# Causal attention with a three-block feed on one Trainium2 core: the order of TensorE's work is planned with a charge for each change of kind, two more slots of probabilities, and the last feed in four streams

## The chip, the core and the metric

One NeuronCore of a Trainium2 chip runs the whole kernel in one launch. The metric is device time in microseconds (us), median of several runs. The core has TensorE (PE, with its weight loads as PEld), VectorE (DVE), ScalarE (ACT), GpSimd (POOL) and SyncE (SP, which here only issues transfers).

## The reference, cut to what matters

`x` is 4096 tokens by 256 channels, float32. The low-rank terms are folded into the weights.

```python
def block(x):
    a = attention(norm(x))            # 16 heads of 16 channels, causal, 4096 keys, then a projection
    x = x + norm(a)
    h = norm(x)
    for m in range(3):                # three blocks of 256x256
        y = gelu(norm(h @ W[2*m].T + b) * gamma + beta)
        h = y @ W[2*m+1].T + b + h
    return x + norm(h)
```

`norm` subtracts the mean of a row and divides by its standard deviation.

## The kernel before, in words

A first part (up to 181 us of the trace) prepares the weights, projects q, k and v, and writes q and k to memory. The change doesn't touch it. The rest is `attend_and_feed`, for which `plan` writes out an order.

**Attention.** There are 8 tiles of 512 tokens (t), each visited once for each of 4 groups of 4 heads: 32 visits. A visit goes through blocks of 128 keys, 576 blocks in all. A block has two *scores* (L904, each two matmuls side by side on 64 rows of the array, written to one of three double banks `S`), two *exps* on ACT (L872, `S` to one of 10 slots of `probs`), a mask by POOL on the diagonal (L859), and one *weigh* (L919: four heads side by side, each 32 columns of the array, summed in the bank `O`). 448 blocks are full; the 128 on the diagonal have 512, 384, 256 or 128 tokens. The trace writes a score as two records and a weigh as eight. After a visit DVE transposes and divides `O` (L1021 to L1032), and SP moves the result to `attT` (L840).

**Feed.** A tile whose four visits are done goes through eleven steps on PE: `project`, `turn_x` (transposes), and for each of three blocks `first`, `turn`, `second`. Each is done for two halves of 256 tokens, k = 0 and 1, in pieces of one matmul of 128x256 (L926, L959, L964, L968; a piece has two records in the trace) or of four transposes (L953). Every step writes the one bank `F`, and DVE must empty it (L1043, L1049, L1055) before the next step's first piece: the halves take turns. Between them DVE takes means and variances (L987, L990), an inverse root in 11 small instructions (`root`, L996 to L1006) and a scaling (L1011); ACT does the GELU on a whole tile (L879), for which it loads another table and then the one for exp again.

**The order.** `plan` is a list scheduler. It gives each item an engine, a time and what it waits for, plays the program through, and picks the ready item with the lowest rank. On PE a score has rank 0, a weigh 1, and a feed piece 0.5 once its due time (counted in scores) has come. The order so found is fixed in each engine's program. The feed of the last tile (t = 7) follows the last weigh, with nothing else beside it: this is called the tail below.

```python
        def urgent(x):
            if e == "PE" and x in due:
                return 0.5 if due[x] <= scores / 2 else 3
            return rank[x]
```

Of the kernel before, what the change touches and what calls it, by code (L numbers as in the profile page):

```python
# [23 lines left out]
P = 128  # L24
# [598 lines left out]
HB = HT // P  # L623
NS, NP = 3, 10
# [10 lines left out]
PIECES = {name: 1 if name.startswith("turn") else 4 for name in STEPS}  # L635
PIECES[STEPS[-1]] = 6
FEED_FROM, FEED_EACH = 26.0, 76.0


def feed_parts():  # L640

    parts = [("x_load", "SP", 1.0, ()), ("evac_att", "DVE", 0.8, ("project",)), ("ln_att", "DVE", 1.3, ("evac_att",)),
             ("rs_att", "DVE", 2.2, ("ln_att",)), ("add_x", "DVE", 1.5, ("rs_att", "x_load")), ("ln_x", "DVE", 1.3, ("add_x",)),
             ("rs_x", "DVE", 2.2, ("ln_x",)), ("norm_x", "DVE", 0.8, ("rs_x",)), ("copy_x", "DVE", 0.8, ("turn_x",))]
    for m in range(BLK):
        out = f"add{m}" if m < BLK - 1 else "evac_h"
        parts += [(f"evac{m}", "DVE", 0.8, (f"first{m}",)), (f"ln{m}", "DVE", 1.3, (f"evac{m}",)), (f"rs{m}", "DVE", 2.2, (f"ln{m}",)),
                  (f"norm{m}", "DVE", 0.8, (f"rs{m}",)), (f"copy{m}", "DVE", 0.8, (f"turn{m}",)), (out, "DVE", 0.9, (f"second{m}",))]  # L650
    return parts + [("ln_h", "DVE", 1.3, ("evac_h",)), ("rs_h", "DVE", 2.2, ("ln_h",)), ("result", "DVE", 1.5, ("rs_h",)), ("store", "SP", 0.5, ("result",))]
# [3 lines left out]
         **{f"turn{m}": f"norm{m}" for m in range(BLK)}, **{f"second{m}": f"gelu{m}" for m in range(BLK)}}  # L655


def plan():
# [3 lines left out]

    parts = feed_parts()
    emptied = {after[0]: name for name, _, _, after in parts if after and after[0] in STEPS}
    feed, due = [], {}
    for t in range(NT):
        mine = [(name, t, k, n) for name in STEPS for k in range(2) for n in range(PIECES[name])]
        feed += mine
        due.update({x: FEED_FROM + FEED_EACH * (t + n / len(mine)) for n, x in enumerate(mine)})
# [6 lines left out]
    for b, (v, t, c, kb, q0) in enumerate(BLOCKS):  # L676
        wide = (TT - q0) / TT
        for n in (2 * b, 2 * b + 1):
            item(("score", n), "PE", 0.02 + 0.213 * wide, [("exp", n - NS) if n >= NS else None, ("score", n - 1) if n else None,
                                                                ("k_load", c), ("q_load", v)], 0)  # L680
            item(("exp", n), "ACT", 0.165 + 0.72 * wide, [("score", n), ("exp", n - 1) if n else None,
                                                                   ("weigh", b - NP // 2) if b >= NP // 2 else None], 1)
# [3 lines left out]
        item(("weigh", b), "PE", 0.12 + 0.86 * wide, [("exp", 2 * b + 1), ("cut", 2 * b + 1) if b in DIAG else None,  # L686
                                                     ("weigh", b - 1) if b else None, ("turn_o", v - 1) if first and v else None], 1)
    for v, (t, i) in enumerate(VISITS):
        item(("turn_o", v), "DVE", 0.8, [("weigh", LAST[v])], 0)
        item(("divide", v), "DVE", 1.7, [("turn_o", v), ("moved", v - 2) if v >= 2 else None], 2)  # L690
        item(("moved", v), "SP", 1.8, [("divide", v)] + [("project", t - AS, k, 3) for k in range(2) if t >= AS], LAST[v])
# [3 lines left out]
    for m, x in enumerate(feed):  # L695
        name, t, k, n = x
        found = [feed[m - 1]] if m else []
        if n == 0:
            if m:
                found.append((emptied[feed[m - 1][0]],) + feed[m - 1][1:3])  # L700
            if name == "project":
                found += [("moved", 4 * t + i) for i in range(NG)]
            elif name.startswith("second"):
                found.append((FEEDS[name], t))
            else:
                found.append((FEEDS[name], t, k))
        item(x, "PE", 0.6 if name.startswith("turn") else 0.432, found, 2)
    for t in range(NT):
        for k in range(2):
            chain = ("result", t - 1, k) if t else None  # L710
            for name, eng, time, deps in parts:
                found = [(a, t, k, PIECES[a] - 1) if a in STEPS else (a, t, k) for a in deps]
                if name == "x_load":
                    found = [("result", t - 2, k) if t >= 2 else None]
                if eng == "DVE":
                    found.append(chain)
                    chain = (name, t, k)
                item((name, t, k), eng, time, found, FEED_FROM + FEED_EACH * t if eng == "SP" else 1 if deps[0] in STEPS else 2)
        for m in range(BLK):
            item((f"gelu{m}", t), "ACT", 4.0, [(f"copy{m}", t, k) for k in range(2)], 0)  # L720
# [12 lines left out]
    scores = 0  # L733
    while len(end) < len(after):
        now, e = min((max(free[e], min(r.values())), e) for e, r in ready.items() if r)

        def urgent(x):
            if e == "PE" and x in due:
                return 0.5 if due[x] <= scores / 2 else 3
            return rank[x]  # L740

        x = min((x for x, at in ready[e].items() if at <= now), key=lambda x: (urgent(x), ready[e][x], str(x)))
        del ready[e][x]
        scores += x[0] == "score"
        end[x] = free[e] = now + us[x]
        found[e].append(x)
        for y in users.get(x, []):
            waiting[y] -= 1
            if not waiting[y]:
                ready[engine[y]][y] = max(end[a] + (0.0 if engine[a] == engine[y] else 2.1 if engine[a] == "SP" else 0.1) for a in after[y])  # L750
# [3 lines left out]
def attend_and_feed(nc, g, d):  # L754
# [4 lines left out]
    order, _ = plan()  # L759

    done = {}
    for e in ("PE", "DVE"):
        total = [0, 0]
        for x in order[e]:
            if len(x) == 3 or len(x) == 4 and x[3] == PIECES[x[0]] - 1:
                total[x[2]] += 1
                done[x[:3]] = total[x[2]]
    place = {x[:3]: n for n, x in enumerate(x for x in order["PE"] if len(x) == 4 and x[3] == 0)}
    gelus = {x: n + 1 for n, x in enumerate(x for x in order["ACT"] if x[0] != "exp")}
    cuts = {n: m + 1 for m, n in enumerate(x[1] for x in order["POOL"])}  # L770

    with ExitStack() as ctx:
        sb = lambda n, s, t=F32: ctx.enter_context(nc.sbuf_tensor(n, s, t))
        sem = lambda n: ctx.enter_context(nc.semaphore(n))
        two = lambda n, s: [sb(f"{n}{k}", s)[(slice(None),) * len(s)] for k in range(2)]
# [10 lines left out]
        xC = sb("xC", [P, 2, 2, HB, C])  # L786
        u, y = two("uC", [P, HB, C]), two("yC", [P, HB, C])
        hT = two("hT", [P, NC, HT])
        st, mv, tmp = two("stC", [P, HB, 6]), two("mvC", [P, HB, 2]), two("tmpC", [P, 3, HB])
        rstd, nmr = two("rstdC", [P, HB]), two("nmrC", [P, HB])  # L790
# [8 lines left out]
        x_in = [[sem(f"x_in{k}{s}") for s in range(2)] for k in range(2)]  # L799
        f_ok, dve_ok, dve_chain, stored = ([sem(f"{n}{k}") for k in range(2)] for n in ("f_ok", "dve_ok", "dve_chainC", "stored"))  # L800
        LOAD = 16 * 2 * PRODUCTS
        x_halves = d["x"][0].rearrange("(t k b p) c -> t k p b c", k=2, b=HB, p=P)
        out_halves = d["out"][0].rearrange("(t k b p) c -> t k p b c", k=2, b=HB, p=P)

        def f_rows():
            return F[:, :].rearrange("p (b c) -> p b c", b=HB)

        def repeated(row):
            return row.unsqueeze(1).to_broadcast([P, HB, C])

        with nc.Block() as block:

            @block.sync
            def _(sp):
                need = sp.value_load(g["need_max"][0:1, 0:1], min_val=0, max_val=1)
                for x in order["SP"]:
# [25 lines left out]
                    elif x[0] == "x_load":  # L842
                        _, t, k = x
                        if t >= 2:
                            sp.wait_ge(dve_ok[k], done["result", t - 2, k])
                        sp.dma_start(xC[:, k, t % 2, :, :], x_halves[t, k]).then_inc(x_in[k][t % 2], 16)
                    else:
                        _, t, k = x
                        sp.wait_ge(dve_ok[k], done["result", t, k])
                        sp.dma_start(out_halves[t, k], y[k]).then_inc(stored[k], 16)  # L850
                for k in range(2):
                    sp.wait_ge(stored[k], 16 * NT)

            @block.gpsimd
            def _(pool):
                for _, n in order["POOL"]:
                    pool.wait_ge(exp_ok, n + 1)
                    tri = probs[:, n % NP, :, 0:P]
                    nc.gpsimd.affine_select(out=tri, in_=tri, compare_op=ALU.is_ge, fill=0.0, base=0,  # L859
                                            pattern=[[0, 2], [1, P]], channel_multiplier=-1).then_inc(cut_ok, 1)  # L860

            @block.scalar
            def _(act):
                for x in order["ACT"]:
# [8 lines left out]
                    else:  # L873
                        m, t = int(x[0][-1]), x[1]
                        for k in range(2):
                            act.wait_ge(dve_ok[k], done[f"copy{m}", t, k])
                        for c in range(NC):
                            col = m * NC + c
                            last = nc.scalar.activation(zT[:, c, :], zT[:, c, :], ACT.Gelu, bias=g["beta"][:, col:col + 1],  # L879
                                                        scale=g["gamma"][:, col:col + 1])  # L880
                        last.then_inc(gelu_ok, 1)

            @block.tensor
            def _(pe):
# [235 lines left out]
```

## Time and profile before

| | |
|---|---|
| median of 3 runs | 1584.68 us (1582.41 to 1588.07) |
| the profiled execution | 1590.69 us, of which its span is 1588.9 us |
| busy in the span | PE 90%, PEld 36%, DVE 40%, ACT 75%, POOL 8% |
| mean granted TensorE clock | 0.939 |
| first score, last weigh, end | 181.4, 1463.6, 1588.9 us |

In rows, a line such as L904 is a line of the kernel before, and "x8" counts records. A time in brackets is idle time of the engine just before the row, with what ended it. PEclk is the granted clock as a share of 2.4 GHz, so 0.5 is 1.2 GHz.

### The profile page before, as it was taken

How to read it: one execution, taken by the hardware profiler on the slowest of the kernel's cores; microseconds unless marked ns; L12 is line 12 of the kernel's file. 1: busy time of each engine (PE TensorE's matmuls, PEld its weight loads, DVE VectorE, ACT ScalarE, POOL GpSimd, SP SyncE). 2: the span in 40 equal slices, each digit the busy share in tenths (PEclk: the TensorE clock that was granted, in tenths of full speed). 3: DMA queues.
4: the chain of work that ended last, by engine and by line, in shares of the span. 5: the costliest groups of instructions: out<-in, count | busy, mean ns of one | idle time of the engine just before them, and what ended most of it. 6: DMA issues, size and time to landing. Idle time of an engine off the chain costs nothing.

```text
span 1588.9 us, 26355 instructions
## 1 busy us (share of the span) xinstructions
PE 1436.3 (90%) x8646; PEld 567.1 (36%) x8646; DVE 638.8 (40%) x2232; ACT 1183.8 (75%) x1370; POOL 131.6 (8%) x355
## 2 busy tenths in 40 slices
PE   6899379999999999999999999999999999998354
PEld 3455123433333333333333333333333333332233
DVE  3376025434633355324531453245332453131635
ACT  1365257888888888888889988888888888888010
POOL 0121122101100000000000000000000000000000
PEclk7699579999999999999999999999999999999666
DMA  5265344445432243223322332223322322210000
GB/s 136 80 211 212 98 103 125 114 113 131 119 79 77 72 101 85 67 69 94 84 71 58 92 97 57 68 77 87 78 71 60 103 61 63 54 32 11 1 0 14
DMA packets 104120, 131.99 MB, mean 83 GB/s; under 512 B 33200, under 2 KB 48560, under 8 KB 103984
## 3 DMA queue, kind: packets, MB, share of 16 engines
q1 hardware_dynamic: 97280, 124.44, 29.3%
q10 hardware_dynamic: 6704, 5.87, 1.3%
q8 instruction: 70, 1.15, 0.3%
q14 instruction: 66, 0.54, 0.1%
HBM read 105.03 MB, written 20.97 MB: 79 GB/s over the span
## 4 chain that ended last, share of the span: by engine, by line
PE 72%; ACT 6%; DVE 5%; SPq 4%; issue 3%; DMA 0%; DVEq 0%; ACTq 0%
PE O L919 29%; PE S L904 23%; PE F L926 10%; PE F L959 4%; SPq L489 3%; ACT probs L872 3%; PE F L953 2%; PE F L964 2%; ACT L872 1%; PE F L968 1%; ACT zT L879 1%; DVE zT L1049 1%; ACT L879 1%; DVE yC L1011 1%; SPq L840 1%
## 5 line engine op out<-in xcount | busy, mean ns | idle before, releaser
L872 ACT ACTIVATE probs<-S 128x1024 f32<-128x1024 f32 (+3 forms) x1152 | 1018.7, 966 | 197.1 <-PE S L904 172.9
L919 PE MATMUL O<-probs,vg 128*32 128x512 f32 (+3 forms) x4608 | 573.5, 576 | 7.2 <-DVE o_turned L1021 4.5
L904 PE MATMUL S<-q_op,k_op 64*128 64x512 f32 (+3 forms) x2304 | 476.9, 455 | 47.5 <-DMA q_op<-qk_rows 27.8
L904 PEld LDWEIGHTS S<-q_op,k_op 64*128 64x128 f32 x2304 | 198.4, 187 | 549.7 <-ACT probs L872 357.3
L859 POOL TENSOR_SCALAR_AFFINE_SELECT probs<-probs 128x256 f32<-128x256 f32 x256 | 103.5, 412 | 1167.9 <-ACT probs L872 1165.5
L1043 DVE TENSOR_TENSOR uC<-F,bffn 128x512 f32<-128x512 f32 x64 | 44.3, 692 | 339.1 <-PE F L926 210.1
L919 PEld LDWEIGHTS O<-probs,vg 128*32 128x32 f32 x4608 | 95.5, 109 | 168.4 <-issue 143.3
L926 PE MATMUL F<-wfT,hT 128*128 128x256 f32 x384 | 129.5, 436 | 6.2 <-DVEq L1044 3.1
L1055 DVE SCALAR_TENSOR_TENSOR hT<-F,b2T,hT 128x256 f32<-128x256 f32 x64 | 28.0, 480 | 184.9 <-PE F L959 184.9
L959 PE MATMUL F<-zT,wfT 128*128 128x256 f32 x256 | 84.6, 445 | 9.2 <-ACT zT L879 6.7
L926 PEld LDWEIGHTS F<-wfT,hT 128*128 128x128 f32 x384 | 63.3, 197 | 53.9 <-issue 39.7
L953 PE MATMUL F<-ident,yC 128*128 128x128 f32 x256 | 44.1, 298 | 36.4 <-DVE yC L1011 36.4
L879 ACT ACTIVATE zT<-zT,beta,gamma 128x512 f32<-128x512 f32 x48 | 36.4, 805 | 51.3 <-DVEq L1051 51.1
L1021 DVE STREAM_TRANSPOSE o_turned<-O 128x512 f32<-128x512 f32 x32 | 22.8, 713 | 118.7 <-PE O L919 118.7
L879 ACT ACT_TABLE_LOAD x22 | 28.2, 1283 | 55.6 <-DVEq L1051 55.4
L987 DVE BATCH_NORM_STATS2 stC<-uC 128x6 f32<-128x256 f32 x160 | 60.1, 418 | 14.4 <-DVEq L1045 13.9
L1011 DVE TENSOR_SCALAR yC<-uC,rstdC,nmrC 128x256 f32<-128x256 f32 x160 | 59.3, 414 | 7.0 <-DVE uC L1043 3.8
L959 PEld LDWEIGHTS F<-zT,wfT 128*128 128x128 f32 x256 | 46.0, 206 | 43.0 <-issue 35.0
L457 PE MATMUL psQ<-xnT,wqkvT 128*128 128x512 f32 x128 | 59.7, 622 | 1.2 <-ACT xnT L341 1.2
L1049 DVE COPY zT<-F 128x512 f32<-128x512 f32 x48 | 33.0, 688 | 65.4 <-PE F L953 65.4
L926 PE MATMUL F<-wpT,attT 128*128 128x256 f32 x128 | 45.5, 448 | 7.2 <-DMA attT<-o_div 6.3
L964 PE MATMUL F<-wfT,zT 128*128 128x256 f32 x128 | 42.3, 432 | 7.6 <-ACT zT L879 6.6
(95 smaller groups left out, 807.0 us busy)
## 6 DMA issues: line engine op xcount, KB each, us to landing
k_op<-qk_rows SPq DMA_DIRECT2D x1152, 64.0 KB, 2.3
qk_rows<-parts SPq DMA_DIRECT2D x32, 512.0 KB, 3.1
q_op<-qk_rows SPq DMA_DIRECT2D x256, 64.0 KB, 2.3
attT<-o_div SPq DMA_DIRECT2D x128, 32.0 KB, 2.0
xC<-in_L_attn_x SPq DMA_DIRECT2D x16, 256.0 KB, 3.1
out<-yC SPq DMA_DIRECT2D x16, 256.0 KB, 2.4
x_in<-in_L_attn_x ACTq DMA_DIRECT2D x6, 512.0 KB, 4.8
q_int<-in_L_ffn_qweights ACTq DMA_DIRECT2D x1, 1536.0 KB, 8.8
```

The lines of the kernel that those rows point to most:

```text
L457: last_mm = nc.tensor.matmul(psQ[:, m, :], g["wqkvT"][:, c, m * P:(m + 1) * P], xnT[:, u, c, :], start=(c == 0), stop=(c == NC - 1))
L859: nc.gpsimd.affine_select(out=tri, in_=tri, compare_op=ALU.is_ge, fill=0.0, base=0, pattern=[[0, 2], [1, P]], channel_multiplier=-1).then_ ...
L872: nc.scalar.activation(probs[:, n % NP, :, 0:TT - q0], S[:, n % NS, :, 0:TT - q0], ACT.Exp, scale=SCALE).then_inc(exp_ok, 1)
L879: last = nc.scalar.activation(zT[:, c, :], zT[:, c, :], ACT.Gelu, bias=g["beta"][:, col:col + 1], scale=g["gamma"][:, col:col + 1])
L904: last = nc.tensor.matmul(S[:, n % NS, a, 0:TT - q0], k_op[mine, c % RING, n % 2, kb % NB * P:(kb % NB + 1) * P], q_op[mine, v % QS, n % 2 ...
L919: last = nc.tensor.matmul(O[h * STRIP:(h + 1) * STRIP, q0:TT], vg[:, kb, col:col + STRIP], probs[:, (2 * b + h // 2) % NP, h % 2, 0:TT - q ...
L926: return nc.tensor.matmul(F[:, b * C:(b + 1) * C], src(c, b), w[:, c, :], start=(c == 0), stop=(c == NC - 1))
L953: last = nc.tensor.transpose(F[:, c * HT + b * P:c * HT + (b + 1) * P], y[k][:, b, c * P:(c + 1) * P], g["ident"][:, :])
L959: last = nc.tensor.matmul(F[:, o * HT:(o + 1) * HT], g["wfT"][:, 2 * m + 1, c, o * P:(o + 1) * P], zT[:, c, k * HT:(k + 1) * HT], start=(c ...
L964: nc.tensor.matmul(F[:, b * C:(b + 1) * C], zT[:, c, tok(b)], g["wfT"][:, 2 * m + 1, c, :], start=(c == 0), stop=False, skip_group_check=True)
L987: last = nc.vector.bn_stats(st[k][:, b, :], src[:, b, :])
L1011: last = nc.vector.tensor_scalar(y[k][:, b, :], src[:, b, :], rstd[k][:, b:b + 1], nmr[k][:, b:b + 1], ALU.mult, ALU.add)
```

## The change

It has three parts.

1. **The planner's rules for PE.** `SWITCH` charges 0.21, 0.13 or 0.2 us when PE's next item is a score, a weigh or a feed piece and the one before it was of another kind; the times of single items lose a part that stood for this. The ranks are replaced: scores are taken when at most `LOW_WATER` = 1 score is ahead of ACT or while a run of scores lasts, a weigh or a feed step that has begun goes on, and a due feed piece waits until two scores are ahead.
2. **Twelve slots of `probs`** for ten, so that exps may be six blocks ahead of the weighs.
3. **The last tile's feed in four streams** of 128 tokens. Stream 0 writes `F`, streams 1 to 3 write one bank each of `S`, which is free by then. A step no longer waits for the bank of another stream. ACT takes over the scaling before a transpose (`norm`) and the copy after it (`copy`); POOL takes over `root` in streams 1 and 3, in 12 instructions; the GELU and the store are done for each stream. The tiles before keep their two halves.

```diff
-NS, NP = 3, 10
+NS, NP = 3, 12
+LOW_WATER, FEED_WATER = 1, 2
+HOP = 0.15
+SWITCH = {"score": 0.21, "weigh": 0.13, "feed": 0.2}
+def parted(t):
+    return 4 if t == NT - 1 else 2
+def runs_on(name, t, k):
+    if name == "store":
+        return "SP"
+    if t == NT - 1 and name.startswith(("norm", "copy")):
+        return "ACT"
+    if t == NT - 1 and name.startswith("rs") and k % 2:
+        return "POOL"
+    return "DVE"
...
-        def urgent(x):
-            if e == "PE" and x in due:
-                return 0.5 if due[x] <= scores / 2 else 3
-            return rank[x]
+        def wish(x):
+            if e != "PE":
+                return rank[x]
+            ahead = scores - sum(1 for z in exp_ends[-8:] if z <= now) - max(0, len(exp_ends) - 8)
+            if x[0] == "score":
+                return 0 if kind == "score" or ahead <= LOW_WATER else 3
+            if x[0] == "weigh":
+                return 1.5 if kind == "weigh" else 2
+            if x[3] and kind == "feed":
+                return 1
+            return 1.8 if due[x] <= scores / 2 and ahead >= FEED_WATER else 4
...
-        end[x] = free[e] = now + us[x]
+        start = now
+        if e == "PE":
+            scores += x[0] == "score"
+            now_kind = x[0] if x[0] in SWITCH else "feed"
+            start += 0.0 if now_kind == kind else SWITCH[now_kind]
+            kind = now_kind
+        end[x] = free[e] = start + us[x]
...
+        def bank(t, k):
+            return F if t < NT - 1 or k == 0 else S[:, k - 1, 0, :]
...
+                    elif name.startswith("norm"):
+                        inputs_done(act, name, t, k)
+                        src = xC[:, t % 2] if name == "norm_x" else u
+                        for b in range(NB)[rows(t, k)]:
+                            last = nc.scalar.activation(y[:, b, :], src[:, b, :], ACT.Identity, bias=nmr[:, b:b + 1], scale=rstd[:, b:b + 1])
+                        last.then_inc(act_ok[k], 1)
+                    else:
+                        inputs_done(act, name, t, k)
+                        dst = hT if name == "copy_x" else zT
+                        nc.scalar.copy(dst[:, :, toks(t, k)], in_channels(t, k)).then_inc(act_ok[k], 1)
```

On PE, where tile 5's first feed block begins amid scores (`S`) and weighs (`O`), the order before goes on, behind the 843rd score:

```order
L919 MATMUL O<-probs,vg 32x512 x4
L904 MATMUL S<-q_op,k_op 128x384 x2
L953 MATMUL F<-ident,yC 128x128 x4
L904 MATMUL S<-q_op,k_op 128x256 x2
L919 MATMUL O<-probs,vg 32x512 x4
L904 MATMUL S<-q_op,k_op 128x256 x2
L904 MATMUL S<-q_op,k_op 128x128 x2
L926 MATMUL F<-wfT,hT 128x256
L904 MATMUL S<-q_op,k_op 128x128 x2
L926 MATMUL F<-wfT,hT 128x256
L904 MATMUL S<-q_op,k_op 128x512 x4
L926 MATMUL F<-wfT,hT 128x256
```

The same place of the order after the change (its lines are L1035 for scores, L1050 for weighs, L1084 and L1098 for the feed):

```order
L1035 MATMUL S<-q_op,k_op 128x512 x6
L1084 MATMUL F<-ident,yC 128x128 x4
L1050 MATMUL O<-probs,vg 32x512 x4
L1035 MATMUL S<-q_op,k_op 128x512 x2
L1035 MATMUL S<-q_op,k_op 128x384 x2
L1098 MATMUL F<-wfT,hT 128x256 x2
L1035 MATMUL S<-q_op,k_op 128x384 x2
L1035 MATMUL S<-q_op,k_op 128x256 x2
L1098 MATMUL F<-wfT,hT 128x256 x2
L1035 MATMUL S<-q_op,k_op 128x256 x2
L1035 MATMUL S<-q_op,k_op 128x128 x4
```

Scores come in twos and threes and feed pieces in twos, where they came one at a time. Over the whole order up to the last weigh, PE begins 802 runs of scores, 530 of weighs and 409 of feed pieces before, and 492, 372 and 230 after the change.

On PE at the end, behind the last weigh, before:

```order
L919 MATMUL O<-probs,vg 32x512 x8
L926 MATMUL F<-wpT,attT 128x256 x8
L953 MATMUL F<-ident,yC 128x128 x8
L926 MATMUL F<-wfT,hT 128x256 x8
L953 MATMUL F<-ident,yC 128x128 x8
L959 MATMUL F<-zT,wfT 128x256 x8
L926 MATMUL F<-wfT,hT 128x256 x8
```

And after the change:

```order
L1050 MATMUL O<-probs,vg 32x512 x8
L1098 MATMUL F<-wpT,attT 128x256 x2
L1098 MATMUL S<-wpT,attT 128x256 x6
L1084 MATMUL F<-ident,yC 128x128 x2
L1098 MATMUL F<-wfT,hT 128x256 x2
L1084 MATMUL S<-ident,yC 128x128 x2
L1098 MATMUL S<-wfT,hT 128x256 x2
L1084 MATMUL S<-ident,yC 128x128 x4
L1098 MATMUL S<-wfT,hT 128x256 x4
```

The streams write different banks, so that one stream's products stand between another's transposes.

## Rows read from the trace of the kernel before

**Rows 1.** The page's chain that ended last, shares of the span by line
```profile
PE O L919 29%; PE S L904 23%; PE F L926 10%; PE F L959 4%; SPq L489 3%; ACT probs L872 3%; PE F L953 2%; PE F L964 2%; ACT L872 1%; PE F L968 1%; ACT zT L879 1%; DVE zT L1049 1%; ACT L879 1%; DVE yC L1011 1%; SPq L840 1%
```
**Rows 2.** Stretches: attention, tail; busy us (records), PEclk, DMA share, GB/s
```profile
core 0: us, PE busy (x) PEld busy (x) DVE busy (x) ACT busy (x) POOL busy (x), PEclk, DMA share, GB/s
181.00:1464.00 1283.00, 1244.98 (x8032) 454.33 (x8032) 493.01 (x1763) 1104.41 (x1236) 103.55 (x256) 0.98 0.32 81
1464.00:1589.00 125.00, 52.94 (x160) 37.60 (x160) 61.46 (x238) 5.83 (x7) 0.00 (x0) 0.64 0.02 6
```
**Rows 3.** Timeline of PE amid attention: start us, us, what
```profile
1299.08 1.13 PE L926 MATMUL F<-wfT,hT 128*128 128x256 f32 x4
1300.14 0.49 PE L904 MATMUL S<-q_op,k_op 64*128 64x512 f32 x2
1300.56 0.70 PE L926 MATMUL F<-wfT,hT 128*128 128x256 f32 x2
1301.19 0.49 PE L904 MATMUL S<-q_op,k_op 64*128 64x512 f32 x2
1301.62 1.07 PE L919 MATMUL O<-probs,vg 128*32 128x512 f32 x8
1302.61 0.49 PE L904 MATMUL S<-q_op,k_op 64*128 64x512 f32 x2
1303.04 1.07 PE L919 MATMUL O<-probs,vg 128*32 128x512 f32 x8
1304.03 0.73 PE L904 MATMUL S<-q_op,k_op 64*128 64x512 f32 x4
...
1352.23 1.92 PE L919 MATMUL O<-probs,vg 128*32 128x512 f32 x16
```
**Rows 4.** Timeline of ACT in the same place
```profile
1304.57 3.77 ACT L872 ACTIVATE probs<-S 128x1024 f32<-128x1024 f32 x4 [0.40 <-PE S L904]
1308.67 2.85 ACT L872 ACTIVATE probs<-S 128x1024 f32<-128x1024 f32 x3 [0.33 <-PE S L904]
```
**Rows 5.** The page's group of exps, and waits: total us, times, longest
```profile
L872 ACT ACTIVATE probs<-S 128x1024 f32<-128x1024 f32 (+3 forms) x1152 | 1018.7, 966 | 197.1 <-PE S L904 172.9
...
ACT probs L872 <- PE S L904: 172.9, 280, 27.4
ACT probs L872 <- PE O L919: 19.8, 19, 2.7
```
**Rows 6.** Timeline of the tail
```profile
1462.52 1.06 PE L919 MATMUL O<-probs,vg 128*32 128x512 f32 x8 [0.75 <-ACT probs L872]
1469.84 3.37 PE L926 MATMUL F<-wpT,attT 128*128 128x256 f32 x8 [6.25 <-DMA attT<-o_div]
1499.41 0.69 DVE L1043 TENSOR_TENSOR uC<-F,bffn 128x512 f32<-128x512 f32 x1 [4.36 <-PE F L926]
1500.34 0.75 DVE L987 BATCH_NORM_STATS2 stC<-uC 128x6 f32<-128x256 f32 x2 [0.24 <-DVEq L1045]
1501.13 0.25 DVE L990 BATCH_NORM_AGGREGATE mvC<-stC 128x2 f32<-128x6 f32 x2
1501.41 0.17 DVE L996 TENSOR_SCALAR tmpC<-mvC 128x2 f32<-128x2 f32 x1
1503.39 0.16 DVE L1006 SCALAR_TENSOR_TENSOR nmrC<-mvC,rstdC 128x2 f32<-128x2 f32 x1
1519.39 0.88 DVE L1055 SCALAR_TENSOR_TENSOR hT<-F,b2T,hT 128x256 f32<-128x256 f32 x2 [7.06 <-PE F L959]
1585.57 0.69 DVE L1074 TENSOR_TENSOR yC<-yC,xC 128x512 f32<-128x512 f32 x1
```
**Rows 7.** Timeline of POOL before attention: first and last of 11 instructions, twice
```profile
32.46 0.20 POOL L82 TENSOR_TENSOR tmpA<-rstdA 128x4 f32<-128x4 f32 x1 [30.93 <-DVE rstdA L112]
35.28 0.20 POOL L95 TENSOR_TENSOR nmrA<-tmpA,rstdA 128x4 f32<-128x4 f32 x1
106.20 0.30 POOL L82 TENSOR_TENSOR tmpA<-rstdA 128x4 f32<-128x4 f32 x1 [6.55 <-DVE rstdA L112]
111.52 0.20 POOL L95 TENSOR_TENSOR nmrA<-tmpA,rstdA 128x4 f32<-128x4 f32 x1 [0.18 <-POOL rstdA L92]
```

More of the change, by code:

```diff
@@ L658, in plan, with gelu_of @@
+def gelu_of(name, t, k):
+    return (f"gelu{name[-1]}", t, k if t == NT - 1 else 0)
 def plan():
     parts = feed_parts()
[L664 removed]
+    emptied = {after[0]: name for name, _, _, after in parts if after[0] in STEPS}
     feed, due = [], {}
     for t in range(NT):
[L667 removed]
+        mine = [(name, t, k, n) for name in STEPS for k in range(parted(t)) for n in range(pieces(name, t))]
@@ L749, in plan @@
             if not waiting[y]:
-                ready[engine[y]][y] = max(end[a] + (0.0 if engine[a] == engine[y] else 2.1 if engine[a] == "SP" else 0.1) for a in after[y])
+                ready[engine[y]][y] = max(end[a] + (0.0 if engine[a] == engine[y] else 2.1 if engine[a] == "SP" else HOP) for a in after[y])
     return found, end
@@ L759, in attend_and_feed @@
     order, _ = plan()
+    parts_after = {name: after for name, _, _, after in feed_parts()}
     done = {}
-    for e in ("PE", "DVE"):
-        total = [0, 0]
+    for e in ("PE", "DVE", "ACT", "POOL"):
+        total = [0] * 4
         for x in order[e]:
-            if len(x) == 3 or len(x) == 4 and x[3] == PIECES[x[0]] - 1:
+            if len(x) == 3 and not x[0].startswith("gelu") or len(x) == 4 and x[3] == pieces(x[0], x[1]) - 1:
                 total[x[2]] += 1
                 done[x[:3]] = total[x[2]]
-    place = {x[:3]: n for n, x in enumerate(x for x in order["PE"] if len(x) == 4 and x[3] == 0)}
-    gelus = {x: n + 1 for n, x in enumerate(x for x in order["ACT"] if x[0] != "exp")}
-    cuts = {n: m + 1 for m, n in enumerate(x[1] for x in order["POOL"])}
+    place = {x[:3]: n for n, x in enumerate(x for x in order["PE"] if len(x) == 4 and x[3] == 0 and x[1] < NT - 1)}
+    gelus = {x: n + 1 for n, x in enumerate(x for x in order["ACT"] if x[0].startswith("gelu"))}
+    cuts = {n: m + 1 for m, n in enumerate(x[1] for x in order["POOL"] if x[0] == "cut")}
     with ExitStack() as ctx:
@@ L854, in _, with link @@
             @block.gpsimd
             def _(pool):
[L856 to L860, printed above, removed]
+                links = [0] * 4
+                def link(k, ins):
+                    links[k] += 1
+                    ins.then_inc(pool_chain[k], 1)
+                    pool.wait_ge(pool_chain[k], links[k])
@@ new lines, in _ @@
+                for x in order["POOL"]:
+                    if x[0] == "cut":
+                        n = x[1]
+                        pool.wait_ge(exp_ok, n + 1)
+                        tri = probs[:, n % NP, :, 0:P]
+                        nc.gpsimd.affine_select(out=tri, in_=tri, compare_op=ALU.is_ge, fill=0.0, base=0,
+                                                pattern=[[0, 2], [1, P]], channel_multiplier=-1).then_inc(cut_ok, 1)
+                    else:
+                        name, t, k = x
+                        inputs_done(pool, name, t, k)
+                        root(t, k).then_inc(pool_ok[k], 1)
@@ L1014, in _, with scaled, emptied @@
+                def scaled(t, k, src):
+                    for b in range(NB)[rows(t, k)]:
+                        last = nc.vector.tensor_scalar(y[:, b, :], src[:, b, :], rstd[:, b:b + 1], nmr[:, b:b + 1], ALU.mult, ALU.add)
+                    return last
+                def emptied(t, k, ins):
+                    link(k, ins)
+                    if t < NT - 1:
+                        dve.sem_inc(f_out, 1)
+                    dve.sem_inc(dve_ok[k], 1)
                 link(0, nc.vector.memset(o_turned[:, :, :], 0.0))
```

312 lines of the change are left out of this document (178 added, 134 removed).

## The prediction, made before the changed kernel had run

> **What bounds the kernel now.** I read the chain that ended last first. Scores and weighs, the work of attention on PE, hold 52% of it and ACT some 4% [rows 1]. The table by stretch then cuts the span in two. In attention, 1283 us long, PE is busy 1245 us, ACT 1104, and the granted clock is 0.98, so PE runs almost always at 2.4 GHz: PE is the bound, with ACT not far behind. In the tail, 125 us, nobody is busy for long: DVE 61 us, PE 53, at a mean clock of 0.64, between 1.2 and 2.4 GHz [rows 2]. There a chain of steps that take turns on one bank is the bound.
>
> What fills PE's 1245 us? The timeline gives it [rows 3]. Four records of scores last 0.73 us and two last 0.49, so a further score costs 0.24 us. Sixteen records of weighs last 1.92 and eight 1.07: 0.85 for a further weigh. Four records of a feed product last 1.13 and two 0.70: 0.43 for a further piece. But the starts lie further apart than that. A score alone is followed 0.43 us after its start (1301.19 to 1301.62), a weigh after 0.99 (1301.62 to 1302.61), a feed piece after 0.63 (1300.56 to 1301.19). So each run, whatever comes next, pays once: 0.19 us for scores, 0.14 for weighs, 0.20 for feed. At these prices the runs of the order before cost 802 x 0.19 + 530 x 0.14 + 409 x 0.20 = 308 us, a quarter of attention.
>
> **Part 1, the planner's rules.** The order loses 310 runs of scores, 158 of weighs and 179 of feed: 58.9 + 22.1 + 35.8 = 117 us. No matmul is added or removed in attention. It lies on the path, since PE is the bound. Two bounds around it: PE is idle or between rows for 38 us of the stretch [rows 2], and if all of that were waits that grow back where a change used to fill them, 79 us would be left. On the upper side the new order may also take some of these waits away, as it holds scores further ahead of need; I allow 10 us and get 127. I take 117, the value of the rows themselves.
>
> Can ACT follow? Its rows cover 1104 us [rows 2]. Exps in a row begin 0.92 us apart (3.77 less 2.85 [rows 4]) though their mean is 0.966 [rows 5], so up to 1152 x 0.046 = 53 us less is needed: 1051 to 1104. The new stretch is 1282 - 117 = 1165 us, so ACT may wait 61 to 114 us in all and hides. It waited 173 us for scores before, in 280 waits [rows 5]. The cover is thin: what is late next, once PE is this fast, is the score for ACT. Behind an ACT wait stand only further exps, and PE's next weigh wants those, so a wait there comes back on PE only when the slots ahead are used up.
>
> The trace and the Trainium skill differ on what a run pays. In the rows the second score, weigh or product of a run pays nothing but its own columns [rows 3]. The page TensorE: Matmul & The Clock Gate, section Part 3: Packing small matmuls, says that a weight load overlaps with matmuls in flight only when its row group differs; every 128-row feed piece and every weigh would then pay for its load, inside a run too, and the second score of a run as well. By the page longer runs would save nothing; by the rows they save all but the first. The sum goes by the rows.
>
> **Part 2, twelve slots.** ACT waited for a weigh to free a slot 19 times, 19.8 us in all [rows 5]. ACT isn't the bound, so I cost this at nothing; its bounds are 0 and a gain of 20 us if ACT should have become the bound. Its work is hidden by PE's 1165 us.
>
> **Part 3, four streams in the tail.** From the end of the last weigh (1462.52 + 1.06 = 1463.6) to the end are 125.3 us. The first 6.3 us, until the first product, stay: DVE divides, SP moves [rows 6]. Now each stream has its own bank, so the wait of one for another's emptying goes, and DVE becomes the engine that all share. Its work, by rows of the tail [rows 6]: an emptying of 512 elements takes 0.69 us and 0.24 until the next instruction; for 256 elements I take 0.45 + 0.24 (a DVE row of 256 from `F` takes 0.88 / 2 = 0.44), 20 of them, 13.8 us. Statistics for one block: half of 0.75, rounded up to 0.42 for the single row, 0.2 for the aggregate and two small instructions at 0.2, with gaps 1.1 us, 24 times: 26.4. A `root` has 11 instructions from 1501.41 to 1503.55, 0.195 apiece; nine remain in it, 1.76 us, 12 times on DVE: 21.1. Two additions of 128 and their wait 0.8 us, 8 times: 6.4. Scaling and adding x, 0.85 us, 8 times: 6.8. Together 74.5 us, more than the 61 of before, for the small instructions cost the same for one block as for two. With 8.4 us before its first emptying (6.3 and two pieces at the low clock, 3.37 / 4 each with a further 0.4) and 2.7 us behind its last (1585.57 + 0.69 to 1588.9), the tail can't be shorter than 86 us.
>
> It will be longer, since POOL's `root` is slow. The nearest rows are the same arithmetic ahead of attention: 11 instructions took 3.0 us with POOL alone (32.46 to 35.48) and 5.5 us beside a busy DVE (106.20 to 111.72) [rows 7]. Twelve instructions are thus 3.3 to 6.0 us against 1.76 on DVE. DVE is the busy engine of the tail, so I take 5.0, nearer to the busy rows. A stream's six roots follow one another: 6 x (5.0 - 1.8) = 19 us on the streams 1 and 3, of which the last ends the kernel. 86 + 19 = 105 us. The bounds are 86 and 125 (no gain). The gain is 20 us, 0 to 39. ACT's added work, 16 scalings, 16 copies and 12 pairs of GELUs, is far below the 80 us in which it had nothing to do; if it were late, DVE's emptyings would wait.
>
> The Trainium skill has a rule against this part. SBUF — State Buffer, section SBUF: two separate sides, says that VectorE and GpSimd share a port pair under an exclusive lock, and the loser waits for the whole instruction. By it DVE's many two-input instructions and POOL's would hold each other up; at its worst the tail would gain nothing. The two timings of rows 7, 3.0 and 5.5 us, agree with such a rule, and the sum already carries a price between them.
>
> **The sum.** 1590.7 (the profiled execution's own time) - 117 - 20 - 0 = 1453.7 us. The median of the runs shown lies 6.0 us lower, so **1447.7 us** against 1584.7, a factor of 0.914.
>
> **The rivals.**
> *A, ACT becomes the bound.* Every one of the 492 runs of scores comes so late that ACT waits 0.33 us, the shorter wait of rows 4. Then attention takes 1104 + 162 = 1266 us, a gain of 16 only, and the kernel 1549 us. For it: scores are now asked for only when at most one is ahead. Against: two or three scores come at a time, and only 280 waits belonged to 802 runs before. Chance 0.08.
>
> *B, slower.* The same place, a larger price: at each run ACT waits 172.9 / 280 = 0.62 us, as in its average wait before [rows 5], because PE is in a weigh (0.99 us) or in four feed pieces (1.9 us) when the last score is being used. Then 1104 + 305 = 1409 us, 127 more than before, less 20 in the tail: 1692 us. It decides from (1282 + 20 - 1104) / 492 = 0.40 us a run. Against: the order puts a score run ahead of other work while ACT still has one in hand, which lasts 0.92 us. Chance 0.03.
>
> *C, a run pays for each of its members.* The price would belong to each weight load and the rows 3 would be a chance pattern; attention stays, the tail gains: 1584.7 - 20 = 1565 us. This is what the rule of TensorE's page comes to. Against: three pairs of rows speak for the first alone. Chance 0.04.
>
> That the change doesn't shorten the runs is excluded by the order itself.
>
> **How the numbers follow.** The forecast has 0.83, A 0.08, C 0.04, B 0.03, and 0.02 are left for what I don't see. Within the forecast, gains of 79 to 127 us and 0 to 39 in the tail reach from 1419 to 1506; both ends at once are unlikely, and the range is 1425 to 1490. A measurement of this kernel can tell about 0.3% (5 us) from no change. All cases but B are faster by more, so faster 0.95, same 0.02, slower 0.03.
>
> **What the profile should show.** Attention from 1282 to about 1165 us at a clock near 1; PE's busy time there down by some 100 us with the same records; the starts behind a run of two scores 0.67 us apart and of three 0.91; ACT over 90% busy with its waits for scores below 114 us. In the tail DVE busy over 70 us of about 105, POOL rows of 0.2 to 0.55 us, and no PE row that waits for another stream's emptying. The forecast is wrong if the runs are longer in the trace and PE's stretch isn't shorter (C), or if ACT's idle time behind scores grows (A, B), or if the tail ends with POOL's instructions on the chain for more than 19 us.

## The result, and the profile after

The changed kernel takes 1453.77 us (median of 4 runs, 1452.23 to 1458.97) against 1586.38 us before: a ratio of 0.917, 95% interval 0.9136 to 0.9204. Forecast were 1447.7 us, or 0.914, in a range of 1425 to 1490. The profiled execution took 1458.97 us with a span of 1457.2, so against the profiled one before (1590.69) it is 131.7 us shorter. 137 had been forecast.

The page's chain that ended last, after the change, answers to [rows 1]. PE's share of weighs and scores went from 52 to 48%, that of ACT's exps (L990) from 3 to 6%.

```profile
PE O L1050 28%; PE S L1035 20%; PE F L1098 9%; ACT probs L990 6%; SPq L489 4%; PE F L1088 2%; PE F L1084 2%; ACT L1000 2%; ACT L990 1%; ACT zT L1000 1%; PE S L1098 1%; PE F L1102 1%; SPq L926 1%; DVE stC L1120 0%; DVE uC L1187 0%
```

The two stretches of the changed kernel, attention and tail, with the columns of [rows 2]:

```profile
181.00:1367.00 1186.00, 1142.98 (x8032) 473.72 (x8032) 494.22 (x1763) 1084.96 (x1236) 103.51 (x256) 0.98 0.35 88
1367.00:1457.00 90.00, 43.82 (x192) 34.59 (x192) 58.79 (x260) 26.04 (x57) 28.09 (x144) 0.75 0.03 8
```

From here on, attention is the time from the first score's start to the start of DVE's last transpose of `O`, and the tail what follows. Attention went from 1282.2 us (181.41 to 1463.66) to 1185.2 (181.66 to 1366.82), 97 less; the tail from 125.2 to 90.4, 35 less. So both parts gained, but not in the shares of the forecast, 117 and 20. In attention PE has the same 8032 records in 102 us less; ACT is busy for 91% of it instead of 86%.

The timeline of PE amid attention after the change, as [rows 3]:

```profile
645.64 0.73 PE L1035 MATMUL S<-q_op,k_op 64*128 64x512 f32 x4
646.31 1.28 PE L1050 MATMUL O<-probs,vg 128*32 128x128 f32 x16
647.52 0.73 PE L1035 MATMUL S<-q_op,k_op 64*128 64x512 f32 x4
648.18 1.13 PE L1098 MATMUL F<-wfT,hT 128*128 128x256 f32 x4
649.25 0.73 PE L1035 MATMUL S<-q_op,k_op 64*128 64x512 f32 x4
649.91 1.92 PE L1050 MATMUL O<-probs,vg 128*32 128x512 f32 x16
651.76 0.96 PE L1035 MATMUL S<-q_op,k_op 64*128 64x512 f32 x6
652.66 1.13 PE L1098 MATMUL F<-wfT,hT 128*128 128x256 f32 x4
653.72 1.06 PE L1050 MATMUL O<-probs,vg 128*32 128x512 f32 x8
654.71 0.99 PE L1035 MATMUL S<-q_op,k_op 64*128 64x512 f32 x6
655.64 1.92 PE L1050 MATMUL O<-probs,vg 128*32 128x512 f32 x16
```

A run of two scores is followed 0.66 us after its start, one of three after 0.90 (651.76 to 652.66), two weighs after 1.85, two feed pieces after 1.06: the prices of [rows 3] again, in the longer runs. One row differs. The three scores at 654.71 last 0.99 and are followed after 0.93: the third had to wait for ACT to leave its bank.

The waits of ACT after the change (total us, times, longest), as the last lines of [rows 5]:

```profile
ACT probs L990 <- PE S L1035: 101.3, 121, 27.4
ACT probs L990 <- PE O L1050: 18.4, 16, 2.7
```

In both kernels the longest of the waits for scores, 27.4 us, lies ahead of the first exp and so outside attention. Inside it ACT waited 145.5 us in 279 waits before, and 73.9 us in 120 waits after.

### The profile page after: what moved, and what is told of

It is laid out like the page before. It is cut to its first block, busy times and chain, and to the rows that moved or that the text cites. A ratio compares the mean times of both kernels' runs of the same rounds, so it can differ in the third digit from the quotient of the medians.

```text
span 1457.2 us, 26427 instructions
## 1 busy us (share of the span) xinstructions
PE 1325.1 (91%) x8678; PEld 583.4 (40%) x8678; DVE 637.3 (44%) x2254; ACT 1184.6 (81%) x1420; POOL 159.6 (11%) x499
## 4 chain that ended last, share of the span: by engine, by line
PE 63%; ACT 10%; issue 5%; SPq 5%; DVE 3%; POOL 1%; DMA 1%; DVEq 0%; ACTq 0%; POOLq 0%
PE O L1050 28%; PE S L1035 20%; PE F L1098 9%; ACT probs L990 6%; SPq L489 4%; PE F L1088 2%; PE F L1084 2%; ACT L1000 2%; ACT L990 1%; ACT zT L1000 1%; PE S L1098 1%; PE F L1102 1%; SPq L926 1%; DVE stC L1120 0%; DVE uC L1187 0%
## 5 line engine op out<-in xcount | busy, mean ns | idle before, releaser
L990 ACT ACTIVATE probs<-S 128x1024 f32<-128x1024 f32 (+3 forms) x1152 | 999.2, 968 | 124.6 <-PE S L1035 101.3
L1050 PE MATMUL O<-probs,vg 128*32 128x512 f32 (+3 forms) x4608 | 539.9, 572 | 5.1 <-DVE o_turned L1163 2.4
L1035 PE MATMUL S<-q_op,k_op 64*128 64x512 f32 (+3 forms) x2304 | 409.8, 435 | 52.0 <-DMA q_op<-qk_rows 30.7
L1035 PEld LDWEIGHTS S<-q_op,k_op 64*128 64x128 f32 x2304 | 188.5, 188 | 426.9 <-ACT probs L990 310.2
L1050 PEld LDWEIGHTS O<-probs,vg 128*32 128x32 f32 x4608 | 111.1, 109 | 211.7 <-issue 187.4
L1187 DVE TENSOR_TENSOR uC<-F,bffn 128x512 f32<-128x512 f32 (+1 forms) x60 | 40.4, 673 | 253.1 <-PE F L1098 143.9
L1098 PE MATMUL F<-wfT,hT 128*128 128x256 f32 x348 | 95.5, 404 | 0.5 <-ACT hT L1012 0.5
L1193 DVE SCALAR_TENSOR_TENSOR hT<-F,b2T,hT 128x256 f32<-128x256 f32 (+1 forms) x60 | 25.7, 470 | 148.5 <-PE F L1088 148.4
L1098 PEld LDWEIGHTS F<-wfT,hT 128*128 128x128 f32 x348 | 60.6, 191 | 29.2 <-issue 21.9
L1088 PE MATMUL F<-zT,wfT 128*128 128x256 f32 (+1 forms) x240 | 63.0, 396 | 6.0 <-ACT zT L1000 5.7
L357 ACT ACTIVATE qf<-psQ,bqk 128x512 f32<-128x512 f32 x32 | 21.9, 684 | 34.4 <-PE psQ L457 33.9
L1084 PE MATMUL F<-ident,yC 128*128 128x128 f32 x232 | 38.6, 288 | 10.2 <-ACT yC L1007 9.9
L1000 ACT ACTIVATE zT<-zT,beta,gamma 128x512 f32<-128x512 f32 (+1 forms) x66 | 42.4, 690 | 0.6
L1098 PE MATMUL F<-wpT,attT 128*128 128x256 f32 x116 | 33.4, 413 | 6.4 <-DMA attT<-o_div 6.3
L1098 PE MATMUL F<-wfT,zT 128*128 128x256 f32 x116 | 35.1, 412 | 3.0 <-ACT zT L1000 2.6
```

Source lines behind the costliest of these rows:

```text
L990: nc.scalar.activation(probs[:, n % NP, :, 0:TT - q0], S[:, n % NS, :, 0:TT - q0], ACT.Exp, scale=SCALE).then_inc(exp_ok, 1)
L1000: last = nc.scalar.activation(zT[:, c, at], zT[:, c, at], ACT.Gelu, bias=g["beta"][:, col:col + 1], scale=g["gamma"][:, col:col + 1])
L1035: last = nc.tensor.matmul(S[:, n % NS, a, 0:TT - q0], k_op[mine, c % RING, n % 2, kb % NB * P:(kb % NB + 1) * P], q_op[mine, v % QS, n % 2 ...
L1050: last = nc.tensor.matmul(O[h * STRIP:(h + 1) * STRIP, q0:TT], vg[:, kb, col:col + STRIP], probs[:, (2 * b + h // 2) % NP, h % 2, 0:TT - q ...
L1084: last = nc.tensor.transpose(into[:, o0:o0 + P], y[:, b, c * P:(c + 1) * P], g["ident"][:, :])
L1088: last = nc.tensor.matmul(into[:, o * wide:(o + 1) * wide], g["wfT"][:, 2 * m + 1, c, o * P:(o + 1) * P], zT[:, c, at], start=(c == 0), st ...
```

## The experiments

The stretches are those of one profiled execution of each kernel, measured as above. Three kernels have the same order of attention and the same exps (changed, root_dve, tail_dve); they lie within 3.0 us of each other there, which tells how exact a stretch is. Each ratio is to executions of the kernel before that go with that kernel (their medians are 1584.5 to 1587.0 us), with its 95% interval.

| kernel | time, us | ratio to before | attention | tail |
|---|---|---|---|---|
| before | 1586.4 | 1 | 1282.2 | 125.2 |
| changed | 1453.8 | 0.917 (0.914 to 0.920) | 1185.2 | 90.4 |
| rules_alone | 1495.7 | 0.943 (0.940 to 0.946) | 1189.6 | 125.4 |
| tail_alone | 1563.2 | 0.985 (0.982 to 0.988) | 1287.9 | 92.5 |
| ten_slots | 1465.8 | 0.924 (0.921 to 0.927) | 1194.5 | 90.5 |
| no_charge | 1508.0 | 0.951 (0.948 to 0.954) | 1234.4 | 89.8 |
| half_exp_before | 1574.2 | 0.992 (0.989 to 0.995) | 1268.5 | 125.5 |
| half_exp_after | 1421.6 | 0.896 (0.893 to 0.899) | 1150.8 | 90.2 |
| root_dve | 1465.5 | 0.924 (0.921 to 0.926) | 1182.7 | 100.8 |
| tail_dve | 1479.7 | 0.932 (0.930 to 0.934) | 1185.7 | 114.0 |
| no_tables | 1426.1 | 0.899 (0.896 to 0.902) | 1154.5 | 89.3 |
| tuned | 1434.1 | 0.904 (0.902 to 0.906) | 1165.0 | 85.9 |

**One part alone: rules_alone.** The kernel before with the charges and the ranks of the change, some other item times of the planner with them.

```diff
-            return rank[x]          # a score 0, a weigh 1, a due feed piece 0.5
+            ...                     # wish(x) and SWITCH of the change
```

> The kernel before with the planner's charges and ranks alone (ten slots, last feed in two halves). PE begins 495 runs of scores, 378 of weighs and 234 of feed before the last weigh, 307, 152 and 175 fewer than before. Price-per-run theory: attention shorter by the 97 us that the change showed, give or take 8, tail as before at 125; about 0.938 of before. Rival (the slots carry part of the gain, ACT waits for slots again): attention gains only 60 to 80, ratio 0.95 or more.

The two stretches of this run:

```profile
180.00:1370.00 1190.00, 1141.72 (x8032) 471.83 (x8032) 492.31 (x1763) 1086.05 (x1236) 103.71 (x256) 0.99 0.34 88
1370.00:1495.00 125.00, 53.14 (x160) 37.72 (x160) 61.24 (x238) 5.83 (x7) 0.00 (x0) 0.64 0.02 6
```

Attention gained 92.6 us, within the 89 to 105 that I had expected, and the tail stayed; the ratio, 0.943, is a little above my 0.938. The rules make nearly all of attention's gain. The range that I gave was the 97 us already measured, give or take 8, and not the price: by the price, 307, 152 and 175 runs fewer are worth 58.3 + 21.3 + 35.0 = 115 us. So this kernel too lacks some 22 us of it, as the changed one lacks 20.

**One part alone: tail_alone.** The changed kernel with the old ranks and item times and ten slots.

```diff
-NS, NP = 3, 12
+NS, NP = 3, 10
...
-        x = min(..., key=lambda x: (wish(x), ready[e][x], str(x)))
+        x = min(..., key=lambda x: (urgent(x), ready[e][x], str(x)))
```

> The changed kernel with the old charges, ranks and ten slots, so only the four streams in the tail are new. Attention as before at 1282 us (within 8), tail 90 us as in the changed kernel; ratio 0.978. Rival (the tail gained because the clock was carried over from a denser attention, not by its streams): tail above 105, ratio above 0.987.

The tail alone:

```profile
1468.00:1560.00 92.00, 46.45 (x192) 33.42 (x192) 59.06 (x260) 26.12 (x57) 28.91 (x144) 0.78 0.03 8
```

It takes 92.5 us behind a slow attention too, so its gain is its own and not that of a denser attention ahead of it. Attention was 5.7 us longer than before, within the 8 us that I had allowed: the old rules wrote a slightly other order here (12 more runs, 1.9 us by their price). The ratio is 0.985 where I had expected 0.978.

**The slots: ten_slots.**

```diff
-NS, NP = 3, 12
+NS, NP = 3, 10
```

> The changed kernel with ten slots of probabilities; the planner writes an order for ten, with 487, 380 and 228 runs. If the slots were worth nothing as forecast: within 0.3% of the changed kernel. If ACT is close to being the bound: 5 to 20 us slower, with more waits of ACT for a weigh than 18 us.

12 us slower than the changed kernel by the medians (8 between the two profiled executions), with intervals that lie apart. Attention is 9.3 us longer. ACT's waits for a weigh grew:

```profile
ACT probs L990 <- PE O L1050: 29.3, 32, 2.5
```

So the slots are worth something, where I had forecast nothing. The number of runs is the same (1095 for 1094): what they buy is room for ACT. How much is less sure. rules_alone has ten slots as well, and its attention is only 4.4 us longer than that of the changed kernel, 2.2 of which its 13 further runs explain. The two pairs put the slots' worth in attention at 2 to 9 us.

**The charge: no_charge.**

```diff
-SWITCH = {"score": 0.21, "weigh": 0.13, "feed": 0.2}
+SWITCH = {"score": 0.0, "weigh": 0.0, "feed": 0.0}
```

> The changed kernel with the three charges at zero, the new ranks kept: 549, 459 and 235 runs, 57, 87 and 5 more than the changed kernel. By the price of a run that is 57 x 0.19 + 87 x 0.14 + 5 x 0.20 = 24 us more. If the order must also know when PE is late, ACT waits more than 101 us for scores, and it is 24 to 80 us slower. Rival (the ranks do it all, the charge is only bookkeeping): within 5 us of the changed kernel.

Attention is 49 us longer. The 149 further runs account for 24 of it, and ACT's waits for scores are longer by 60:

```profile
ACT probs L990 <- PE S L1035: 161.7, 251, 27.3
```

The ranks by themselves give half of attention's gain (48 of 97 us); the other half needs a planner that knows when PE will really be free. One place of the trace shows how the order fails without it. Behind one of ACT's GELUs, PE waits for ACT ahead of two single scores. In the plan's own reckoning the exps that these scores wait for had ended before PE came free:

```profile
801.24 0.38 PE L1035 MATMUL S<-q_op,k_op 64*128 64x256 f32 x2 [0.50 <-ACT probs L990]
801.94 0.33 PE L1035 MATMUL S<-q_op,k_op 64*128 64x128 f32 x2 [0.32 <-ACT probs L990]
```

**Where the missing 20 us are: half_exp_before and half_exp_after.** In both kernels an exp works on half of its columns, and what it leaves out keeps what the slot held (1.0 at the start). PE's instructions and their order stay as they are.

```diff
-nc.scalar.activation(probs[:, n % NP, :, 0:TT - q0], S[:, n % NS, :, 0:TT - q0], ACT.Exp, scale=SCALE)
+nc.scalar.activation(probs[:, n % NP, :, 0:(TT - q0) // 2], S[:, n % NS, :, 0:(TT - q0) // 2], ACT.Exp, scale=SCALE)
...
+nc.vector.memset(probs[:, :, :, :], 1.0)     # once, ahead of attention
```

> The kernel before, each exp over half of its columns only (the other half of the probabilities is a constant), so ACT cannot be late. TensorE's instructions and their order are those of before. If PE's list is the bound of attention: attention loses little, from 1282 to 1255 to 1275 us. Rival (ACT's waits and PE's are one loop and the exps were the bound in places): below 1240.

> The changed kernel with the same half exps. If the price of a run (0.19, 0.14, 0.20 us) is right, the difference between this and half_exp_before in attention is 117 us, 20 more than with whole exps, since the 20 missing are waits for ACT: attention near 1145 to 1155 us. Rival (the missing 20 lie in PE's own list or in the transfers at the start): the difference stays near 97.

Attention of the kernel before, then of the changed one, each with half exps:

```profile
180.00:1449.00 1269.00, 1238.73 (x8032) 451.65 (x8032) 491.25 (x1763) 689.96 (x1236) 102.76 (x256) 0.99 0.33 82
```

```profile
182.00:1333.00 1151.00, 1121.15 (x8032) 466.58 (x8032) 494.29 (x1763) 661.47 (x1236) 101.63 (x256) 0.98 0.37 90
```

ACT is busy for some 670 us instead of 1100. Attention falls to 1268.5 and to 1150.8 us, both within what I had expected. Their difference is 117.7 us, and the price of the runs had given 117. PE's records alone show it as well: 1238.73 less 1121.15 is 117.6. So close a match is in part luck: the prices are rounded to 0.01 us, which for 647 runs leaves 3 us either way. With whole exps 97 are left, since ACT costs the order before 14 us and the new one 34.

**What of ACT it is: no_tables.** The identity stands where the GELU stood, which needs no other table.

```diff
-last = nc.scalar.activation(zT[:, c, at], zT[:, c, at], ACT.Gelu, ...)
+last = nc.scalar.activation(zT[:, c, at], zT[:, c, at], ACT.Identity, ...)
```

> The changed kernel with the identity in place of the GELU (the GELU itself is left out), so ACT loads no table for it: 42 loads of 1.28 us, 54 us, go from ACT's 1085 in attention, at the same order of PE. If ACT is the bound in places: attention falls by a part of the 34 us that half exps gave, 10 to 30 us. Rival (a table load is hidden in the slots ahead): less than 5 us.

Attention is 30.7 us shorter, just above the 10 to 30 that I had expected and nearly the 34 that half exps gave. The group in question, from the timeline of ACT in the changed kernel:

```profile
631.58 1.28 ACT L1000 ACT_TABLE_LOAD   x1
632.88 1.52 ACT L1000 ACTIVATE zT<-zT,beta,gamma 128x512 f32<-128x512 f32 x2
634.41 1.28 ACT L990 ACT_TABLE_LOAD   x1
635.71 16.31 ACT L990 ACTIVATE probs<-S 128x1024 f32<-128x1024 f32 x20
652.30 11.34 ACT L990 ACTIVATE probs<-S 128x1024 f32<-128x1024 f32 x12 [0.29 <-PE S L1035]
```

21 times ACT leaves the exps for 4.13 us (631.58 to 635.71), 2.56 of it loads. After this pause it works through 20 exps with no wait: it is behind, and PE's order is then held to ACT's pace. Behind the 21 pauses there are 6 to 23 such exps, 12 in the median; in the kernel before, whose pauses are as long, 3 to 10, 8 in the median.

Whether the loss arises there can be read off row by row, since the changed kernel, half_exp_after and no_tables have the same 8032 records of PE in the same order. Take the 21 stretches from the beginning of a pause to the end of its exps without a wait, 313 us of attention in all. In them the changed kernel falls behind no_tables by 31.3 us, and in all the rest by nothing (it regains 0.6). Behind half_exp_after it falls by 29.5 of the 34.4 us in them. So nearly the whole loss arises behind the pauses.

**The tail, engine by engine: root_dve and tail_dve.** In root_dve the roots of streams 1 and 3 are on DVE; in tail_dve the scalings and copies as well.

```diff
-    if t == NT - 1 and name.startswith(("norm", "copy")):     # left out in tail_dve only
-        return "ACT"
-    if t == NT - 1 and name.startswith("rs") and k % 2:       # left out in both
-        return "POOL"
```

> The changed kernel with the roots of streams 1 and 3 in the tail on DVE too, none on POOL. Attention has the same order. If DVE is what the streams share, its 12 further roots of 1.76 us (21 us) lengthen the tail from 90 to 100 to 111 us. Rival (the chain of a stream bounds, and POOL's 3.3 us for a root only delay it): tail 80 to 90.

> The changed kernel with roots, scalings and copies of the tail all on DVE: only four streams with banks of their own are left of its third part. DVE then has 21 us of roots, 16 scalings of 0.45 and 16 copies of 0.65 us more, 39 us in all. If DVE is the shared bound: tail 120 to 130 us, as long as before, and the streams by themselves are worth nothing. Rival (the banks are the gain): tail 90 to 105.

The tail of root_dve, then of tail_dve:

```profile
1364.00:1464.50 100.50, 46.60 (x192) 35.42 (x192) 74.10 (x368) 26.59 (x57) 0.00 (x0) 0.73 0.02 7
```

```profile
1366.00:1479.00 113.00, 54.09 (x192) 41.61 (x192) 85.92 (x400) 10.31 (x24) 0.00 (x0) 0.66 0.02 6
```

POOL's help is worth 10 us: 15 us more of DVE work (59 to 74) lengthened the tail by 10.4, to 100.8, at the lower edge of the 100 to 111 expected if DVE is what the streams share. ACT's help is worth 13 (12 us of DVE work). The four streams, each with its own bank, GELU and store, bring the remaining 11, from 125 to 114. For tail_dve neither expectation held: it lies between 105 and 120. So the streams by themselves are worth something, but two thirds of the tail's gain come only when ACT and POOL take work off DVE. What isn't separated is TensorE's clock. In the tail it is 0.64 before, 0.66 in tail_dve, 0.73 in root_dve and 0.75 in the changed kernel, and it matters: in the tail before, four products (8 records) take 3.75 us at a granted clock of 0.50 (from 1515.51) and 1.99 us at 1.00 (from 1525.19). A part of each gain may be the clock's.

**A faster one: tuned.**

```diff
-NS, NP = 3, 12
+NS, NP = 3, 14
-FEED_FROM, FEED_EACH = 26.0, 76.0
+FEED_FROM, FEED_EACH = 30.0, 78.5
-    if t == NT - 1 and name.startswith("rs") and k % 2:
+    if t == NT - 1 and name.startswith("rs") and k < 3:
```

> The changed kernel with fourteen slots, the feeds due later (from block 30, 78.5 blocks a tile, for 26 and 76), and the roots of streams 0, 1 and 2 on POOL in the tail. PE begins about as many runs (493, 373, 229), so the price of runs gives no gain. If ACT's waits are what is left over the price (20 us and more), later feeds and more slots take part of them away: attention 1165 to 1180 us for 1185, tail 86 to 90. Rival (PE's list alone bounds): attention within 4 us of the changed kernel.

```profile
181.00:1347.00 1166.00, 1132.52 (x8032) 471.26 (x8032) 488.47 (x1745) 1083.92 (x1236) 104.42 (x256) 0.99 0.32 89
1347.00:1432.00 85.00, 43.95 (x192) 33.76 (x192) 54.98 (x225) 26.35 (x57) 42.18 (x216) 0.76 0.04 12
```

1434.1 us, ratio 0.904: faster than both kernels. Attention is 20 us shorter than in the changed kernel with as many runs (1095), at the lower edge of what I had expected, and the tail 4.5 us. ACT's waits for a weigh are down to 5.0 us:

```profile
ACT probs L990 <- PE O L1050: 5.0, 7, 1.1
```

How the 20 us divide between slots and later feeds wasn't tried, nor whether the tail's 4.5 us are those of the third root on POOL.

## Why the prediction was right, and where it was not

**The bound and the price of a run: right.** PE bounds attention, and a run pays 0.19, 0.14 or 0.20 us once. The half exps show 117.7 us where the sum had 117, and the rows of the changed kernel show the same starts: two feed pieces are followed after 1.06 us, one after 0.63. By that, rival C is out for these shapes. The rule behind it, that of the Trainium skill (TensorE: Matmul & The Clock Gate, section Part 3: Packing small matmuls) that a weight load overlaps with matmuls in flight only when its row group differs, doesn't hold for them either. The same section also lets a load run ahead into a background weight buffer, which the prediction left out; the rows fit that case.

**"ACT may wait 61 to 114 us in all and hides": wrong in part.** It stayed off the chain for the most part, but took 34 us instead of the 14 it had taken before, so 97 us were gained and not 117. The term was inside its bounds (79 to 127). The step that failed was to compare totals: in attention ACT waited 92 us in all (73.9 for scores, 18.4 for slots), well inside the 61 to 114, and still cost PE 34. ACT's pauses of 4.13 us at the GELUs are longer than four exps, with three banks of scores in between, and with PE faster ACT needs 12 exps (in the median) instead of 8 to catch up. Whether a fourth bank would help wasn't tried. Rivals A and B had the place right, ACT behind PE's list, but not the manner: A had a late score at each of the 492 runs, 162 us in all, and B 305 us. There were 120 waits in attention, of 73.9 us. The 173 us from which B took its 0.62 us a wait also held the 27.4 us ahead of attention; without them it is 145.5 / 279 = 0.52, and B would have attention at 1361 us, still slower than before.

**"I cost this at nothing" (the slots): wrong, by 2 to 9 us in attention.** The argument was that ACT isn't the bound. It isn't on average, but it is for the stretch behind each pause. That the slots count just there fits this, but isn't shown. The bound of 20 us held.

**The tail: right mechanism, the size off by 15 us.** 105 us were forecast and 90.4 measured. That the wait for another stream's bank goes and DVE is left as what the streams share shows in DVE's waits for PE in the tail, 52 us before and 14 after, of which 7.4 and 6.1 stand ahead of the first emptying. The longest of them, before and after:

```profile
DVE hT L1055 <- PE F L959: 20.8, 4, 7.1
DVE uC L1043 <- PE F L926: 18.1, 5, 7.4
```

```profile
DVE uC L1187 <- PE F L1098: 8.0, 3, 6.1
DVE uC L1187 <- PE S L1098: 3.5, 4, 1.2
```

Two terms were too large. The timelines of DVE and POOL in the tail of the changed kernel:

```profile
1421.24 0.42 DVE L1187 TENSOR_TENSOR uC<-S,bffn 128x256 f32<-128x256 f32 x1 [0.89 <-PE S L1098]
1421.82 0.43 DVE L1120 BATCH_NORM_STATS2 stC<-uC 128x6 f32<-128x256 f32 x1
1422.28 0.18 DVE L1123 BATCH_NORM_AGGREGATE mvC<-stC 128x2 f32<-128x6 f32 x1
1422.49 0.15 DVE L1126 TENSOR_SCALAR tmpC<-mvC 128x1 f32<-128x1 f32 x1
1422.68 0.15 DVE L1127 TENSOR_SCALAR rstdC<-tmpC 128x1 int32<-128x1 int32 x1
1422.75 0.41 DVE L1187 TENSOR_TENSOR uC<-F,bffn 128x256 f32<-128x256 f32 x1
```

```profile
1415.92 0.20 POOL L955 TENSOR_TENSOR tmpC<-rstdC 128x1 f32<-128x1 f32 x1 [6.03 <-DVE rstdC L1127]
1416.20 0.19 POOL L956 TENSOR_TENSOR tmpC<-tmpC 128x1 f32<-128x1 f32 x1
...
1418.72 0.22 POOL L965 TENSOR_SCALAR tmpC<-mvC 128x1 f32<-128x1 f32 x1
1419.03 0.19 POOL L966 TENSOR_TENSOR nmrC<-tmpC,rstdC 128x1 f32<-128x1 f32 x1
```

A root on POOL takes 3.3 us (1415.92 to 1419.22), not 5.0: ten us less on six roots of a stream. DVE needs 0.58 for an emptying and 0.93 for the statistics, for 0.69 and 1.1 in the sum: 20 x 0.11 + 24 x 0.17 = 6 us less. With both, 105 becomes 89. The same sum with all roots on DVE is 86 + 21 - 6 = 101 us, and root_dve has 100.8. DVE was busy for 59 us of the 90, where the forecast wanted over 70 of 105: its sum of 74.5 also held the gaps between small instructions, 9 us in the trace from the first emptying on. The two errors of the forecast, 20 us too much in attention and 15 too little in the tail, nearly cancelled; the total was closer than its terms.

Beside a busy DVE, POOL was slow ahead of attention in the kernel before, and hardly ever in the tail of the changed one. DVE's share isn't the reason: it was busy for 77% of the slow root of rows 7 (106.20 to 111.72) and for 69% of the twelve roots on POOL in the tail, 83% beside the one shown. Its instructions were others. The DVE rows beside the slow POOL rows, in the kernel before:

```profile
106.01 0.43 DVE L406 TENSOR_SCALAR parts<-qf 128x512 int32<-128x512 int32 x1
106.48 0.69 DVE L409 TENSOR_TENSOR parts<-qf,parts 128x512 f32<-128x512 f32 x1
```

```profile
106.68 0.55 POOL L83 TENSOR_TENSOR tmpA<-tmpA 128x4 f32<-128x4 f32 x1 [0.18 <-POOL tmpA L82]
```

POOL's row ends at 107.23, when the 0.69 us of L409 with two inputs from SBUF have ended at 107.17. In the tail 142 of POOL's 144 rows take 0.19 to 0.22 us, beside DVE's root rows of 0.16 us and also beside its rows of statistics of 0.43 (26 of POOL's rows, all 0.19). The other two stand beside a scaling and an addition of 128x256:

```profile
1444.50 0.41 DVE L1145 TENSOR_SCALAR yC<-uC,rstdC,nmrC 128x256 f32<-128x256 f32 x1
1444.94 0.43 DVE L1210 TENSOR_TENSOR yC<-yC,xC 128x256 f32<-128x256 f32 x1
```

```profile
1444.60 0.36 POOL L959 TENSOR_TENSOR tmpC<-rstdC 128x1 f32<-128x1 f32 x1
1445.04 0.38 POOL L960 TENSOR_TENSOR tmpC<-tmpC 128x1 f32<-128x1 f32 x1
```

Again each ends 0.05 us after DVE's row. This agrees with the rule of the Trainium skill (SBUF — State Buffer, section SBUF: two separate sides), by which the loser waits for the whole instruction of the winner. I should have asked which DVE rows stand beside POOL's, and not how busy DVE is: a wait for a whole instruction costs at most what that instruction lasts, and most of DVE's rows in the tail cost nothing.

## What to carry to other kernels

Price a change of kind on TensorE by subtraction in the timeline: the start of the next run, less the start of this one, less its items at their marginal cost. Multiplied with the count of runs, it told within 3 us, the rounding of the prices, what longer runs give where ACT is never late. A planner that is told this price wrote a better order here than one that is only told to prefer runs (attention 1185 against 1234 us). Before such a gain is taken at full value, look for the pauses of the next engine, and compare the longest of them, not the mean load, with what the buffers between the two cover.

## What the runs showed of the hardware that I had not expected

A pair of table loads on ACT, 2.56 us, costs attention 1.5 us per GELU (30.7 us over 21), though ACT was idle for 8% of the time. And a small POOL instruction beside a busy DVE takes 0.2 us or up to 0.55, by which instruction DVE runs: its root rows of 0.16 us and its statistics rows of 0.43 us don't hold it up, while an addition of two inputs from SBUF of 0.43 or 0.69 us does where it began first, until that row has ended.
